# Softplus sums on TensorE and three of sixteen drives on GpSimd in a selective scan, Trainium2

## The reference, cut to what matters

```
delta = softplus(dts + dt_bias)                      # per channel and position
def step(h, inp):
    d_t, x_t, B_t, C_t = inp
    dA = exp(d_t[..., None] * As)                    # decay
    h = dA * h + (d_t * x_t)[..., None] * B_t[...]   # drive
    y = einsum('bkdn,bkn->bkd', h, C_t)
    return (h, y)
```

## Time and profile before

| | us |
|---|---|
| median of 3 runs | 838.02 |
| profiled execution | 838.86 |
| its span | 837.1 |
| TensorE busy | 656.1 (78%) |
| VectorE busy | 624.1 (75%) |
| GpSimd busy | 423.9 (51%) |
| ScalarE busy | 348.3 (42%) |

### The profile page before, as it was taken

The page is one execution under the profiler, slowest core; times in us unless marked ns, Lnnn a source line. Parts: engine busy times, 40 slices in busy tenths (PEclk is TensorE's granted clock), DMA queues, the critical chain, the costliest instruction groups (busy, mean ns, idle before and its releaser), DMA issues. The chain is left out here.

```text
span 837.1 us, 6603 instructions
## 1 busy us (share of the span) xinstructions
PE 656.1 (78%) x2268; PEld 333.3 (40%) x2268; DVE 624.1 (75%) x603; ACT 348.3 (42%) x379; POOL 423.9 (51%) x231
## 2 busy tenths in 40 slices
PE   2878878788787877888777677666575769999997
PEld 2442222222222322222222222244324557777775
DVE  5298999999999899999999849755693154443432
ACT  3485465374653744646435126123003223332331
POOL 5039979999899899999987510000051000000000
PEclk9989899999999999999999887889596579999999
DMA  5043543545443535435454342210730000000000
GB/s 163 3 151 131 169 156 138 185 142 167 163 140 128 177 140 187 155 126 176 154 177 166 109 169 107 69 41 0 271 131 0 1 0 1 1 1 0 0 0 26
DMA packets 27229, 88.36 MB, mean 106 GB/s; under 512 B 3637, under 2 KB 4375, under 8 KB 26463
## 3 DMA queue, kind: packets, MB, share of 16 engines
q1 hardware_dynamic: 27200, 88.01, 30.3%
HBM read 86.87 MB, written 1.13 MB: 105 GB/s over the span
## 5 line engine op out<-in xcount | busy, mean ns | idle before, releaser
L578 POOL TENSOR_TENSOR area<-area 128x1024 f32<-128x1024 f32 x127 | 298.8, 2368 | 75.6 <-DVE area L1091 54.6
L1091 DVE TENSOR_TENSOR_SCAN area<-area,ps 128x1024 f32<-128x1024 f32 x128 | 289.4, 2274 | 0.0
L1374 PE MATMUL ps<-area,cst 128*128 128x512 f32 x512 | 258.8, 630 | 1.5 <-POOL area L578 1.1
L757 ACT ACTIVATE area<-area,floors,par_sb 128x1024 f32<-128x1024 f32 x128 | 158.1, 1239 | 177.3 <-DVE area L1091 174.9
L1084 DVE TENSOR_TENSOR ps<-ps,area 128x1024 f32<-128x1024 f32 x128 | 154.3, 1211 | 7.7 <-PE ps L1353 7.2
L1374 PEld LDWEIGHTS ps<-area,cst 128*128 128x128 f32 x512 | 89.2, 192 | 109.4 <-issue 101.9
L1353 PE MATMUL ps<-stack,sel 32*128 32x512 f32 x256 | 64.7, 503 | 68.2 <-DVE area L1091 64.0
L1626 PE MATMUL ps<-stack,sel 128*128 128x512 f32 (+1 forms) x576 | 116.5, 363 | 0.4 <-DVE sel L1275 0.4
L1626 PEld LDWEIGHTS ps<-stack,sel 128*128 128x128 f32 x576 | 97.2, 191 | 19.6 <-issue 1.2
L438 DVE COPY area<-ps 64x1024 f32<-64x1024 f32 x32 | 39.3, 1227 | 73.8 <-PE ps L1642 41.4
L1353 PEld LDWEIGHTS ps<-stack,sel 32*128 32x128 f32 x256 | 23.9, 184 | 160.8 <-DVE area L1091 135.9
(11 more groups left out here) (285 smaller groups left out, 650.0 us busy)
## 6 DMA issues: line engine op xcount, KB each, us to landing
area<-c_rows SPq DMA_DIRECT2D x128, 512.0 KB, 3.7
area<-phi_scaled SPq DMA_DIRECT2D x1, 4104.0 KB, 25.3
area<-in_m_phi_dram SPq DMA_DIRECT2D x4, 1024.0 KB, 8.5
area<-phi_scaled SPq DMA_DIRECT2D x1, 4096.0 KB, 15.0
area<-in_q_t_dram SPq DMA_DIRECT2D x1, 1024.0 KB, 14.0
area<-in_dft_dram SPq DMA_DIRECT2D x1, 784.0 KB
area<-in_m_u_dram SPq DMA_DIRECT2D x1, 768.0 KB, 6.1
area<-in_conv_w_dram SPq DMA_DIRECT2D x1, 576.0 KB, 6.6
```

Source lines behind the costliest of these rows:

```text
L578: pool.tensor_tensor(scan_order(prod[:, u % PRODS, :], k), lines(state[:, u % STATES, :], k), lines(c_sb[:, u % COPIES, :], k), MUL).then_ ...
L757: act.activation(decay[:, u % DECAYS, :], delta[:, n % 2, :], ACT.Exp, bias=floors[:, k, i:i + 1], scale=par_sb[:, k, i:i + 1]).then_inc(s ...
L1091: dve.tensor_tensor_scan(state[:, u % STATES, :], decay[:, u % DECAYS, :], drive_pair(u), 0.0, MUL, ADD).then_inc(sig("scanned"), 1)
L1374: mm = pe.matmul(ps[:, 6 + h, :], con("center"), half(prod[:, u % PRODS, :], h), start=False, stop=(u % (UNITS // 2) == UNITS // 2 - 1), s ...
```

## The change

1. *Softplus sums.* GpSimd's three sums go. A new job `soft` on TensorE adds the four terms into a bank pair by products with the identity, one half after its own slot is free, the other half after the next slot's spread. ScalarE copies the result in scan order to delta. GpSimd keeps the product delta * x, now after unit 10 (12 in block 0).
2. *Aided units.* Units 1, 7 and 12 of blocks 1 to 6 and 1, 5, 9 and 12 of block 7 (22 in all) get no spread and no drive on VectorE. SyncE writes the B rows to DRAM beside the C rows and brings the unit's B row, broadcast, into the buffer `aid`; GpSimd multiplies it by delta * x three units ahead. ScalarE writes that unit's decay into the bank pair of its slot, and the scan reads decay from PSUM and drive from SBUF. The decay buffers go from 4 to 3, which makes room for `aid`.
3. *Places.* z before unit 3, rows before 6, soft before 9 (block 0: 5, 8, 11); ScalarE's softplus steps two units earlier; `first_image(0)` in the turn of unit 66. Some semaphores are merged.

```diff
-        DECAYS, STATES, PRODS, COPIES = 4, 4, 3, 3
+        DECAYS, STATES, PRODS, COPIES = 3, 4, 3, 3
+        aid = take(L)
...
-            JOB_BEFORE[NS * _n + 5] = ("z", _n + 1)
-            JOB_BEFORE[NS * _n + 9] = ("rows", _n + 1)
+            _first = NS * _n + (5 if _n == 0 else 3)
+            JOB_BEFORE[_first] = ("z", _n + 1)
+            JOB_BEFORE[_first + 3] = ("rows", _n + 1)
+            JOB_BEFORE[_first + 6] = ("soft", _n + 1)
+        AIDED = [NS * _n + _i for _n in range(1, BLOCKS) for _i in ((1, 7, 12) if _n < BLOCKS - 1 else (1, 5, 9, 12))]
...
+            def b_row_in(v):
+
+                at = AIDED.index(v)
+                if at:
+                    sp.wait_ge(sig("scanned"), AIDED[at - 1] + 1)
+                n, i = divmod(v, NS)
+                sp.wait_ge(sig("c_rows_out"), 32 + 64 * n)
+                sp.dma_start(aid, c_dram.ap()[n, 0, i:i + 1, :].broadcast_to([P, L])).then_inc(sig("b_in"), 16)
...
+                if u + 3 in AIDED:
+                    b_row_in(u + 3)
...
+            def aid_drive(v):
+
+                n, at = v // NS, AIDED.index(v)
+                pool.wait_ge(sig("u_ready"), n + 1)
+                pool.wait_ge(sig("b_in"), 16 * (at + 1))
+                pool.tensor_tensor(aid, aid, u_in[:, n % 2, :], MUL).then_inc(sig("pool_driven"), 1)
...
+                if u + 3 in AIDED:
+                    aid_drive(u + 3)
...
-                act.activation(decay[:, u % DECAYS, :], delta[:, n % 2, :], ACT.Exp, bias=floors[:, k, i:i + 1],
+                if u in AIDED:
+                    kind, before = slots[slots.index(("a", u)) - 3]
+                    act.wait_ge(sig(FREED[kind]), before + 1)
+                    dst = banks(BANK["a", u])
+                else:
+                    wait(act, sig("scanned"), u - DECAYS + 1)
+                    dst = decay[:, u % DECAYS, :]
+                act.activation(dst, delta[:, n % 2, :], ACT.Exp, bias=floors[:, k, i:i + 1],
...
+                elif kind == "soft":
+                    k = i % ND
+                    act.wait_ge(sig("soft_done"), i)
+                    wait(act, sig("decayed"), NS * (i - 1))
+                    act.activation(lines(delta[:, i % 2, :], k), scan_order(banks(BANK["soft", i]), k),
+                                   ACT.Copy).then_inc(sig("delta_ready"), 1)
...
+                if u in AIDED:
+                    dve.wait_ge(sig("pool_driven"), AIDED.index(u) + 1)
+                    dve.tensor_tensor_scan(state[:, u % STATES, :], banks(BANK["a", u]), aid, 0.0,
+                                           MUL, ADD).then_inc(sig("scanned"), 1)
...
-                if early and u + 1 < UNITS:
+                if early and u + 1 < UNITS and u + 1 not in AIDED:
                     drive_unit(u + 1)
                 scan_unit(u)
-                if not early:
+                if not early and u + 1 not in AIDED:
                     drive_unit(u + 1)
...
+            def soft_terms(n, h):
+
+                pe.wait_ge(sig("log_ready"), n + 1)
+                pe.wait_ge(sig("rest_ready"), n + 1)
+                for at, term in enumerate((tz, te, tw, ta)):
+                    mm = pe.matmul(ps[:, BANK["soft", n] + h, :], ident, half(term, h), start=(at == 0), stop=(at == 3))
+                if h == 1:
+                    mm.then_inc(sig("soft_done"), 1)
...
                 if kind == "b":
                     spread_b(i)
-                else:
+                elif kind == "soft":
+                    soft_terms(i, 0)
+                elif kind != "a":
                     job(kind, i)
-                if slots[at - 3][0] == "b":
+                if slots[at - 1][0] == "soft":
+                    soft_terms(slots[at - 1][1], 1)
+                if slots[at - 3][0] in ("a", "b"):
                     scanned = slots[at - 3][1]
-                if i >= 4 or kind != "b":
+                if (i >= 4 or kind != "b") and kind != "soft":
                     for u in range(done, min(done + 2, scanned - LAG + 1)):
                         sum_state(u)
                         done = u + 1
```

More of the change, by code:

```diff
@@ L297, in program @@
                 slots.append(JOB_BEFORE[_u])
-            slots.append(("b", _u))
+            slots.append(("a" if _u in AIDED else "b", _u))
         BANK = {turn: 2 * (at % 3) for at, turn in enumerate(slots)}
         BANK["z", 0], BANK["rows", 0], BANK["gate", 1] = 4, 2, 6
-        FREED = {"z": "relu_ready", "b": "scanned", "rows": "rows_rounded", "gate": "z_ready", "spec": "spec_out",
+        FREED = {"z": "relu_ready", "b": "scanned", "a": "scanned", "soft": "delta_ready", "rows": "rows_rounded", "gate": "z_ready", "spec": "spec_out",
                  "skip": "skip_copied", "var": "var_logged"}
@@ L304, in program, with own_drives @@
         OUT_AT, VAR_AT = BANK["b", UNITS - 3], BANK["b", UNITS - 2]
+        def own_drives(u):
+            return u - sum(v < u for v in AIDED)
         def drive_pair(u):
@@ L507, in c_rows_out @@
                 src = c_raw(n)
[L508 to L511, removed]
+                for what in ((0, 1) if n else (1,)):
+                    for h in range(2):
+                        at = 64 * what + 32 * h
+                        sp.dma_start(c_dram.ap()[n, what, :, h * HALF:(h + 1) * HALF],
+                                     src[at:at + NS, :]).then_inc(sig("c_rows_out"), 16)
+            def b_row_in(v):
[5 more added lines that the diff above has]
+                sp.dma_start(aid, c_dram.ap()[n, 0, i:i + 1, :].broadcast_to([P, L])).then_inc(sig("b_in"), 16)
             c_rows_out(0)
@@ new lines, in soft_sum @@
+            def soft_sum(n):
+                b, k = divmod(n, ND)
+                pool.wait_ge(sig("delta_ready"), n + 1)
+                wait(pool, sig("driven"), own_drives(NS * (n - 1)))
+                pool.tensor_tensor(lines(u_in[:, n % 2, :], k), lines(delta[:, n % 2, :], k),
+                                   scan_order(xc[:, b, :], k), MUL).then_inc(sig("u_ready"), 1)
+            def aid_drive(v):
[3 more added lines that the diff above has]
+                pool.tensor_tensor(aid, aid, u_in[:, n % 2, :], MUL).then_inc(sig("pool_driven"), 1)
@@ L604, in split_rows, with pair_sum @@
             def split_rows(n):
                 pool.wait_ge(sig("rows_masked"), n)
-                wait(pool, sig("b_spread"), NS * (n - 1))
+                wait(pool, sig("b_spread"), own_drives(NS * (n - 1)))
                 pool.tensor_tensor(b_rows[:, n % 2, :], rows_raw[0:64], rows_mask[0:64], ADD).then_inc(sig("rows_ready"), 1)
-            def pair_sum(t, made, name):
-                pool.wait_ge(sig(made), 1)
-                pool.tensor_tensor(t[:, 0:HALF], t[:, 0:HALF], t[:, HALF:L], ADD).then_inc(sig(name), 1)
+            def pair_sum(t, made):
+                pool.wait_ge(sig("spec_act"), made)
+                pool.tensor_tensor(t[:, 0:HALF], t[:, 0:HALF], t[:, HALF:L], ADD).then_inc(sig("spec_pool"), 1)
@@ L737, in rows_round @@
                 if n:
-                    wait(act, sig("c_rows_out"), 32 * n)
+                    wait(act, sig("c_rows_out"), 64 * n - 32)
                 src = ps[:, BANK["rows", n], :]
@@ L855, in _ @@
                     serve(*SERVED[u])
-                if i == 3 and n < BLOCKS - 1:
+                if i == (3 if n == 0 else 1) and n < BLOCKS - 1:
                     soft(n + 1, "exp")
                     soft(n + 1, "one_plus")
-                elif i == 4 and n < BLOCKS - 1:
+                elif i == (4 if n == 0 else 2) and n < BLOCKS - 1:
                     soft(n + 1, "log")
@@ L878, in _ @@
                     weigh_ident()
+                if (n, i) == (4, 2):
+                    first_image(0)
             for h in range(2):
@@ L1141, in _ @@
             dve.wait_ge(sig("signed"), 2)
[L1142 removed]
+            dve.wait_ge(sig("spec_pool"), 4)
             recurrence(dve, link)
```

72 lines of the change are left out of this document (24 added, 48 removed).

## The result

| | before | changed |
|---|---|---|
| median us | 838.15 (4 runs, 837.76 to 839.49) | 865.49 (4 runs, 863.35 to 867.8) |
| profiled execution / its span | 838.86 / 837.1 | 864.44 / 862.6 |
| first scan starts / last scan ends | 47.35 / 477.64 | 45.7 / 503.5 |

The ratio is 1.0324 with a 95% interval of 1.0292 to 1.0355: 3.2% slower. The forecast was 862, 23.6 us more than before; the medians differ by 27.3, the two profiled executions by 25.6.

What follows compares the result with a forecast made beforehand. VectorE was taken to bound the scan stage: 399.1 us of work plus waits made 453.9 against 430.3, so 23.6 more, 838.0 to about 862 us. Forecast 856 to 868 (62%); wider range 850 to 876.

Steps and rivals of the forecast that it cites:

- Drives removed: VectorE in the scan stage: 22 of 128 drives leave at 1.12 us each, 24.6 us, aided scans no slower.
- The soft jobs: TensorE between scan 6 and spread 10 (block 0: same order, later units): VectorE waits 5.2 us a job, seven jobs 36.6 us.
- Jobs before unit 13: Extra TensorE jobs in blocks 1, 2, 3 and 5: spreads 0.3 and 1.2 us late, 4.5 us, plus 1.1 in block 5.
- Block 4: Sum 64 waits for ScalarE's later copies of y, so the spread for drive 5 comes 6.8 us late.
- rival 5: TensorE's clock drops to 1.2 GHz at one or two soft jobs, 7 us longer each: 869 to 876 us, chance 8%.
- GpSimd's extras: Blocks 3 to 5: extra GpSimd work makes product 15 and aided products late, 2.5 us together, ends 0 and 8.
- The start: The wait before the second of the first sums stays: 2.15 + 1.11 = 3.3 us.
- 1: Rival: TensorE's soft job is covered between scan 6 and spread 10, so the kernel gets faster: about 818 us, chance 5%.
- 2: Rival: the soft job's identity products run in one record, 0.43 us each, seven waits total 11.4: 836 us, chance 3%.
- 3: Rival: small waits don't form, only soft jobs cost, late-spread terms are halved and GpSimd's are nothing: 853 us, chance 10%.
- 4: Rival: GpSimd also becomes the bound, TensorE late again, 8 to 12 us on top: 872 us, chance 12%.
- for it: by load TensorE has 5 us to spare: Argument for the rival of a covered soft job: by load alone TensorE has 5 us spare per block.

Runs made afterwards that it cites:

- e1: The changed kernel with no unit aided, VectorE driving all 128, softplus sums still on TensorE: 880.69 us, ratio 1.0495 to the kernel before.
- e3: The changed kernel with no state sums in TensorE's turn behind the soft slot, they follow in the next turn: 858.45 us, ratio 1.022 to the kernel before.
- e4: The changed kernel with VectorE running scan 9 ahead of drive 10 (block 0: scan 11 ahead of drive 12): 859.88 us, ratio 1.0243 to the kernel before.
- e2: The changed kernel with two of the soft job's four terms left out, 4 products instead of 8: 852.31 us, ratio 1.0156 to the kernel before.
- e11: The changed kernel with the first image's y copied and squared in the turn of unit 65 instead of 66: 862.41 us, ratio 1.0267.
- e5: The changed kernel's 22 aided units alone, softplus sums on GpSimd and jobs in their old places: 865.99 us, ratio 1.0312 to the kernel before.
- e8: The changed kernel reordered: soft job's second half split, state sums later, some GpSimd products and the y copies earlier: 852.24 us, ratio 1.0151.
- e9: The kernel before with six aided units (three decay buffers), softplus sums on GpSimd, jobs in old places: 832.70 us, ratio 0.9926.
- e6: The changed kernel with the decay of aided units in SBUF instead of PSUM: 905.18 us, ratio 1.0768 to the kernel before.
- e10: As e8, with one state sum put ahead of the soft job's first half: 847.41 us, ratio 1.0122 to the kernel before.

## Why the prediction was right, step by step

- *Drives removed, 24.6 us.* 22 drives of 1.12 us from start to start are gone. VectorE's busy time in the stage fell by 22.5, which is not the same measure: neighbouring records overlap by about 0.1 us. The aided scans cost 2278 ns: nothing added.
- *The soft jobs, 36.6 us.* Measured 5.10 + 4.83 + 5.10 + 4 x 5.11 = 35.5. The place, the queue order and the product's price (3.55 a half) are as worked out. e1 (waits kept without aided units), e3 and e4 (waits moved by order alone) show the mechanism. e2 shows one step missing in it, the wait of spread 9 for scan 7, which did not change this sum.
- *Jobs before unit 13, 4.5 + 1.1.* Measured 1.11 + 1.12 + 1.11 and 1.11, so 4.5: the second part (1.2 forecast) is near, the first (0.3 each) did not form.
- *Block 4, 6.8.* Measured 1.41 + 6.10 = 7.5. ScalarE's chain ended 14.7 us after scan 0 began, for 14.9 forecast. The skip products then took 3.5 us, not 1.72. The clock in that place, and in two more of the kernel after where two products take longer than the usual 1.81 us (same columns as above):

```profile
120.32:123.92 3.60, 3.60 (x8) 1.17 (x4) 3.60 (x2) 1.79 (x3) 0.61 (x1) 0.53 0.50 196
290.99:294.50 3.51, 3.51 (x4) 1.51 (x5) 0.00 (x0) 1.08 (x1) 0.83 (x1) 0.51 1.01 331
348.14:351.00 2.86, 2.86 (x5) 0.82 (x6) 1.01 (x1) 2.83 (x4) 2.86 (x2) 0.66 0.58 175
```

  The granted clock is 0.51 at 290.99, nearly all at the lower of the two levels, after TensorE had stood 3.7 us for ScalarE. This is rival 5 in other places than I put it: the soft jobs ran at full clock.
- *GpSimd's extras, 2.5.* This term was the one mis-sized: 2.68 + 1.13 us at the starts of blocks 5 and 6, 0.68 + 0.40 + 0.25 at aided scans (the 0.25 for ScalarE's decay), and 0.54 + 0.40 late spreads in block 1 that I had not seen; 6.1 in all, within the 0 to 8 given. Not all of that is GpSimd's. The two waits of block 1 stand right behind the slow sum at 120.32; e2 and e4 run the same sum at full clock (118.99:120.91 in e2: 1.00) and have neither wait. At the start of block 5 the kernel after has the slow sum at 348.14 and waits 2.68; e11 and e4 run it at full clock after the same wait of 1.7 us for GpSimd, and wait 1.43 and 1.45. In e11:

```profile
349.85 1.98 PE L1414 MATMUL ps<-area,cst 128*128 128x512 f32 x4 [1.71 <-POOL area L598]
```

  So about 0.9 + 1.2 us of this term are the clock's, by estimate, and about 4 us of the whole sum with the 1.8 of the skip products. The forecast had put the clock into a rival, not into the sum.
- *The start, 3.3*: 2.15 + 1.11.
- *Sum.* Waits 56.9 us for 54.8 forecast. That the two are so near is in part luck: without the clock's some 4 us it would have been about 53, with the soft jobs and the jobs before unit 13 each forecast 1.1 too high. 399.1 + 56.9 = 456.0, and 1.8 us that no wait in the list accounts for give the 457.8. Against this the first scan starts 1.65 us earlier in this execution and what follows the last scan is 0.4 shorter, neither of which was forecast. 27.5 - 2.0 = 25.5, as the spans differ; the forecast was 23.6.
- *Rivals.* 1 and 2 (covered, or one record) fall by the 3.55 us halves. 3 falls, the small waits formed. 4 lay behind the soft waits (GpSimd catches up in them) and came out in e3, e5 and e8. The reason of "for it: by load TensorE has 5 us to spare" was true and without effect.

## What to carry to other kernels

When work is moved to an engine with spare load, write down that engine's queue between the event that releases the new work and the next result the bound engine needs, and compare the two lengths; busy shares did not show it here. In this kernel, with three engines busy 82 to 87% of the stage and coupled by rings of 3 or 4 buffers, taking one wait away (e3, e8) uncovered the next. The gain that was found lay in moving only as much as the helper has idle time in that very block (e9): six drives instead of 22, with the softplus sums and all jobs in their old places.

## What was not expected of the hardware

- A scan with both operands in SBUF beside a busy GpSimd takes 3.89 us in the mean instead of 2.28, and up to 8.93 where GpSimd has three instructions in a row; GpSimd's strided product takes 4.29 instead of 2.58 (e6). ScalarE writing the decay to PSUM takes 1.21 us, to SBUF 1.24.
- In the kernel after TensorE waits 3.70 us for ScalarE's copies of y and then runs the two skip products in 3.5 us instead of 1.72, at a granted clock of 0.51, so nearly all at the 1.2 GHz level of the two (1.2 and 2.4). In e11 sum 63, after a wait of 1.71 us for GpSimd, takes 3.58 us instead of 1.81. A wait of TensorE in a busy stage can so be paid twice. It need not: in the kernel after the sum at 284.87, behind a wait of 1.70 us, runs at a granted clock of 1.00, and the slow sum at 120.32 has only a wait of 1.18 and a rows job before it.
- Some changed orders scatter more than the kernel before (837.76 to 839.49): 863.35 to 867.8 for the change, 844.08 to 852.97 for e10. Others do not (e4: 858.91 to 860.06). The time goes with the granted clock of the whole run: 0.930 in the two faster and 0.922 in the two slower runs of the change, 0.936 in e10's fastest and 0.917 in its slowest. Why the clock differs from run to run is open.
